# A new order for the head of a fused state-space, mixture-of-experts and attention kernel

## The reference, cut to what matters

```python
xn = layernorm(x)                                  # rows of 128
# layer 0: a long convolution plus a top-2 mixture of experts, both on xn
K  = 2 * Re(sum_n Ct[h,n] * exp(dtA[h,n] * l))     # filter of 1024 taps from log_A_real, A_imag, C, log_dt
y  = irfft(rfft(xn, 2L) * rfft(K, 2L))             # convolution over the sequence
a  = layernorm(xn + y + xn * D) * ln_w + ln_b
logits = xn @ Wg.T                                 # 8 experts, the best two are kept, softmax over the two
m  = sum over the two chosen experts e of gate_e * W3[e] @ (silu(W1[e] @ xn) * (W2[e] @ xn))
x  = x + a + m
# layer 1: attention and a dense mixture of 8 experts on layernorm(x)
x  = x + attention(layernorm(x)) + experts(layernorm(x))
```

## Time and profile before

| what | value |
|---|---|
| time, median of 3 runs | 822.92 us (822.19 to 824.34) |
| span of the profiled execution | 820.2 us |
| what lies around the span, against the median | 2.7 us |
| PE busy | 757.8 us, 92% |
| DVE busy | 658.9 us, 80% |
| ACT busy | 550.4 us, 67% |
| POOL busy | 146.5 us, 18% |
| chain that ended last | PE 75%, POOL 9%, DVE 8%, issue 4%, ACT 3% |

### The profile page before, as it was taken

One profiled execution on the slowest core, in us unless ns is written; L12 is line 12 of the kernel. 1 busy time (PEld: TensorE's weight loads), 2 busy tenths in 40 slices (PEclk: granted clock), 3 DMA queues, 4 the chain that ended last, 5 costly groups with the idle time before them and its releaser, 6 DMA issues.

```text
span 820.2 us, 11626 instructions
## 1 busy us (share of the span) xinstructions
PE 757.8 (92%) x3893; PEld 615.2 (75%) x3893; DVE 658.9 (80%) x1558; ACT 550.4 (67%) x939; POOL 146.5 (18%) x138
## 2 busy tenths in 40 slices
PE   6956366999999998999999999999999999999998
PEld 6624255888888645868788878887888887999997
DVE  7699767899937689998799889976777778877775
ACT  5833123344434368898999899889999997665663
POOL 0067775000000254643044000000000000000000
PEclk9978659899999999999999999999999999999999
DMA  8834582689876512413033112211211210000000
GB/s 251 347 104 137 185 285 90 200 250 289 291 223 195 163 40 70 86 54 89 15 102 81 40 38 59 47 43 44 55 45 49 52 27 0 14 14 20 14 20 27
DMA packets 81274, 85.15 MB, mean 104 GB/s; under 512 B 7361, under 2 KB 59841, under 8 KB 80961
## 3 DMA queue, kind: packets, MB, share of 16 engines
q1 hardware_dynamic: 77120, 76.04, 31.3%
q0 software_dynamic: 4096, 8.40, 3.5%
HBM read 59.12 MB, written 25.30 MB: 103 GB/s over the span
## 4 chain that ended last, share of the span: by engine, by line
PE 75%; POOL 9%; DVE 8%; issue 4%; ACT 3%; DMA 1%; SPq 0%; DVEq 0%; POOLq 0%
PE ps L1829 19%; PE ps L1831 18%; PE ps L1830 18%; POOL x_slots L643 9%; PE ps L1948 6%; PE ps L2024 3%; PE ps L2171 3%; DVE hid_lo L1755 2%; PE ps L1842 1%; PE ps L1927 1%; PE ps L2198 1%; PE ps L1869 1%; PE ps L1848 1%; DVE xn L1436 1%; ACT L880 1%
## 5 line engine op out<-in xcount | busy, mean ns | idle before, releaser
L1755 DVE TENSOR_TENSOR hid_lo<-hid,hid_hi 128x512 fp32r<-128x512 f32 x256 | 175.3, 686 | 52.1 <-ACT hid_hi L881 49.5
L880 ACT ACTIVATE hid<-ps,b_sb 128x512 f32<-128x512 f32 x256 | 177.7, 694 | 36.7 <-PE ps L1831 18.8
L881 ACT ACTIVATE hid_hi<-ps,b_sb 128x512 fp32r<-128x512 f32 x256 | 176.0, 688 | 0.0
L1829 PE MATMUL ps<-hid_hi,w_lo 128*128 128x512 f32 x256 | 102.1, 399 | 5.4 <-DVE hid_lo L1755 5.2
L1829 PE MATMUL ps<-xt_hi,w_lo 128*128 128x512 f32 x256 | 102.4, 400 | 1.5 <-DVE xn L1428 1.5
L1831 PE MATMUL ps<-xt_hi,w_hi 128*128 128x512 f32 x256 | 99.9, 390 | 0.0
L1831 PE MATMUL ps<-hid_hi,w_hi 128*128 128x512 f32 x256 | 99.8, 390 | 0.0
L1830 PE MATMUL ps<-xt_lo,w_hi 128*128 128x512 f32 x256 | 99.8, 390 | 0.0
L1830 PE MATMUL ps<-hid_lo,w_hi 128*128 128x512 f32 x256 | 99.8, 390 | 0.0
L792 ACT ACTIVATE act<-ps 128x512 f32<-128x512 f32 (+1 forms) x57 | 34.0, 596 | 81.6 <-PE ps L1831 81.6
L643 POOL DMA_INDIRECT x_slots<-xn,slot x64 | 71.4, 1115 | 62.6 <-DVE expert_of L1158 43.4
(11 more groups left out here) (337 smaller groups left out, 1543.9 us busy)
## 6 DMA issues: line engine op xcount, KB each, us to landing
gate_row<-gates_dram SPq DMA_DIRECT2D x64, 256.0 KB, 4.8
wc<-w_split SPq DMA_DIRECT2D x57, 256.0 KB, 3.7
w_split<-wc SPq DMA_DIRECT2D x8, 768.0 KB, 4.1
x_slots<-prod SPq DMA_DIRECT2D x11, 512.0 KB, 9.7
xc<-x_slots SPq DMA_DIRECT2D x19, 256.0 KB, 4.3
y_slots<-yo SPq DMA_DIRECT2D x19, 256.0 KB, 4.1
wst<-w SPq DMA_DIRECT2D x16, 256.0 KB, 4.7
wd<-w SPq DMA_DIRECT2D x19, 192.0 KB, 3.1
```

What stands on the lines that cost most here:

```text
L880: nc.scalar.activation(hid1[:, u % 4], ps[:, u % 4], ACT.Gelu_apprx_tanh, bias=b1_sb[:, u:u + 1])
L881: nc.scalar.activation(hid1_hi[:, u % 4], ps[:, u % 4], ACT.Gelu_apprx_tanh, bias=b1_sb[:, u:u + 1]).then_inc(hid1_done, 1)
L1755: tt(hid1_lo[:, u % 4], hid1[:, u % 4], hid1_hi[:, u % 4].bitcast(F32), sub).then_inc(hid1_lo_done, 1)
L1829: mm(dst, a_lo, b_hi, start=first, stop=False)
```

## The change

The instructions are the same; their order in the head differs, four waits are split or loosened, and six loads go to another queue.

- SP issues the eight groups of x first, then fwd0, then the zeros over x_slots, then the two raw expert weights, then the zeros over y_slots (with a semaphore of their own, spare_out), then the two small weights.
- ACT issues the small loads itself, before anything else: wg0, the two halves of log_dt, the state parameters, wqk, consts, prefix.
- PE: the product of wqk goes from the second group to behind the ranks; four numbers of spectra instead of three stand ahead of the routing's matmuls, and these no longer wait for ws_lo.
- ACT: four xt_copy before root0(0); the normalising of groups 2 to 4 follows all copies and root0(1); the filter's tanh, exp and sines go behind the gates' exponential.
- DVE: six groups of moments before scale0(0); expm1_start behind the moments; the polynomial (expm1_series) behind the choice of experts; the slots follow directly; then expm1_rest, discretise, the gates, discretise_rest.
- POOL: the scatter waits for the zeros of x_slots alone, for slots_done of 1, and group by group for the normalised rows.

The core of the diff:

```diff
@@ sync
-            for half in range(2):
-                sp.dma_start(ks[half * N:(half + 1) * N, 0, :],
-                             log_dt[half * HH:(half + 1) * HH].partition_broadcast(N)).then_inc(small_in, 16)
-            sp.dma_start(small[:], state_params).then_inc(small_in, 16)
-            sp.dma_start(wg0_sb[:], wg0).then_inc(wg0_in, 16)
             for g in range(G):
                 sp.dma_start(rows3(g), group(x, g)).then_inc(group_in[g], 16)
-                if g == 1:
-                    sp.dma_start(wqk_sb[:], wqk_t).then_inc(wqk_in, 16)
...
-            for e in range(2):
-                w0_load(e)
             sp.wait_ge(blank_done, 1)
...
+            for e in range(2):
+                w0_load(e)
...
-                         ).then_inc(blanks_out, 16)
+                         ).then_inc(spare_out, 16)
@@ gpsimd
-            pool.wait_ge(blanks_out, 16 * (-(-NC // 2) + 1))
-            pool.wait_ge(slots_done, 3)
-            pool.wait_ge(xn_ready, G)
+            pool.wait_ge(blanks_out, 16 * -(-NC // 2))
+            pool.wait_ge(slots_done, 1)
             for t in range(T):
+                if t % B == 0:
+                    pool.wait_ge(xn_ready, t // B + 1)
@@ scalar
+            act_e.dma_start(wg0_sb[:], wg0).then_inc(wg0_in, 16)
...
+            for g in range(4):
+                xt_copy(g)
             root0(0)
+            xt_copy(4)
+            normalise0(0)
+            xt_copy(5)
+            normalise0(1)
+            xt_copy(6)
+            xt_copy(7)
+            root0(1)
+            for g in range(2, 5):
+                normalise0(g)
+            spectrum_copy(0)
+            normalise0(5)
+            act_e.wait_ge(counted, 1)
...
@@ vector
-            expm1_start()
-            for g in range(5):
+            for g in range(6):
                 moments0(g, signal=(g == 3))
             scale0(0)
...
-            expm1_rest()
+            expm1_start()
             scale0(1)
...
             tt(m2, m2, m1, sub).then_inc(top2_done, 1)
-            discretise()
-            dve.wait_ge(top2_exp_done, 1)
...
+            expm1_series()
             dve.wait_ge(ranked, 1)
...
+            expm1_rest()
+            discretise()
+            dve.wait_ge(top2_exp_done, 1)
...
+            discretise_rest()
+            dve.wait_ge(ws_hi_done, 1)
@@ tensor
-                if g == 1:
-                    pe.wait_ge(wqk_in, 16)
-                    mm(ps[:, 4, 0:P], wqk_sb[:, 0], wqk_sb[:, 1], start=True, stop=True).then_inc(qk_mm, 1)
...
+            pe.wait_ge(wqk_in, 16)
             pe.wait_ge(fwd0_in, 16)
-            spectra(range(3))
+            spectra(range(4))
             pe.wait_ge(member_done, 1)
-            pe.wait_ge(ws_lo_done, 1)
...
+            mm(ps[:, 4, 0:P], wqk_sb[:, 0], wqk_sb[:, 1], start=True, stop=True).then_inc(qk_mm, 1)
-            spectra(range(3, 16))
+            spectra(range(4, 16))
```

More of the change, by code:

```diff
@@ L270, in program @@
         blanks_out = sem("blanks_out")
+        spare_out = sem("spare_out")
         member_done = sem("member_done")
@@ L528, in _ @@
                 down_load(e, q)
-            sp.wait_ge(blanks_out, 16 * (-(-NC // 2) + 1))
+            sp.wait_ge(blanks_out, 16 * -(-NC // 2))
+            sp.wait_ge(spare_out, 16)
             sp.wait_ge(blocks_known, 1)
@@ L706, in spectrum_copy @@
                 copy(z[:, m + HM * odd, c, part_], ps[:, n % 4]).then_inc(spectra_copied, 1)
[L708 to L711, removed]
-            root0(0)
-            for g in range(2, 4):
-                xt_copy(g)
-            for g in range(4):
-                normalise0(g)
-                xt_copy(g + 4)
-            root0(1)
+            act_e.dma_start(wg0_sb[:], wg0).then_inc(wg0_in, 16)
+            for half in range(2):
+                act_e.dma_start(ks[half * N:(half + 1) * N, 0, :],
+                                log_dt[half * HH:(half + 1) * HH].partition_broadcast(N)).then_inc(small_in, 16)
+            act_e.dma_start(small[:], state_params).then_inc(small_in, 16)
+            act_e.dma_start(wqk_sb[:], wqk_t).then_inc(wqk_in, 16)
+            act_e.dma_start(consts[:], lag_row.partition_broadcast(P)).then_inc(route_in, 16)
+            act_e.dma_start(prefix_sb[:], prefix).then_inc(route_in, 16)
+            for g in range(4):
+                xt_copy(g)
+            root0(0)
+            xt_copy(4)
[6 more added lines that the diff above has]
+            for g in range(2, 5):
+                normalise0(g)
+            spectrum_copy(0)
+            normalise0(5)
+            act_e.wait_ge(counted, 1)
+            copy(counts[:], ps[:, 6, 0:2 * P].rearrange("p (a t) -> p a t", a=2)).then_inc(counts_copied, 1)
+            for g in range(6, G):
+                normalise0(g)
+            for n in range(1, 4):
+                spectrum_copy(n)
+            act_e.wait_ge(top2_done, 1)
+            nc.scalar.activation(p2, m2, ACT.Exp).then_inc(top2_exp_done, 1)
             act_e.wait_ge(decay_done, 1)
@@ L724, in _ @@
             nc.scalar.activation(ks[:, 8], ks[:, 12], ACT.Sin, scale=TWO_PI / 2).then_inc(trig_done, 1)
-            for g in range(4, 6):
-                normalise0(g)
-            for n in range(2):
+            for n in range(4, 6):
                 spectrum_copy(n)
[L729 to L736, removed]
+            act_e.wait_ge(qk_mm, 1)
+            copy(ws_hi[:], ps[:, 4, 0:P]).then_inc(ws_hi_done, 1)
             act_e.wait_ge(ws_in, 32)
@@ L765, in _ @@
                 spectrum_copy(n)
-            act_e.wait_ge(blanks_out, 16 * (-(-NC // 2) + 1))
+            act_e.wait_ge(blanks_out, 16 * -(-NC // 2))
+            act_e.wait_ge(spare_out, 16)
             for c in range(KC):
@@ L990, in expm1_start, with expm1_series @@
                 need(v)
-            def expm1_rest():
+            def expm1_series():
                 v = step.mark(ts(PP, R, 1.0 / math.factorial(7), None, mul))
@@ L997, in expm1_rest @@
                     v = step.mark(stt(PP, PP, 1.0 / math.factorial(k), R, add, mul))
+            def expm1_rest():
+                need(step.n)
                 power = exp2[:].rearrange("p (a h) -> p a h", a=2)
@@ L1072, in discretise_rest @@
                 v = step.mark(ts(K(21), K(19), -1.0, None, mul))
-            expm1_start()
-            for g in range(5):
+            for g in range(6):
                 moments0(g, signal=(g == 3))
             scale0(0)
-            for g in range(5, G):
+            for g in range(6, G):
                 moments0(g, signal=(g == G - 1))
-            expm1_rest()
+            expm1_start()
             scale0(1)
-            dve.wait_ge(ws_hi_done, 1)
-            tt(ws_lo[:], ps[:, 4, 0:P], ws_hi[:].bitcast(F32), sub).then_inc(ws_lo_done, 1)
             wide = lambda a: a.unsqueeze(2).broadcast_to((P, T, E))
@@ L1089, in _ @@
             v = step.mark(tt(eq, means, wsum, mul))
-            need(v)
+            need(step.n)
             dve.wait_ge(route_in, 32)
@@ L1166, in _ @@
             ts(first_blocks[:], R_(2)[:, BLOCKS:BLOCKS + 1], 1.0, None, add).then_inc(blocks_known, 1)
+            expm1_rest()
+            discretise()
+            dve.wait_ge(top2_exp_done, 1)
+            v = step.mark(ts(p1, p2, 1.0, None, add))
+            need(v)
+            v = step.mark(nc.vector.reciprocal(p1, p1))
+            need(v)
+            step.mark(tt(gate2[:], p2, p1, mul))
+            step.mark(nc.vector.tensor_copy(xn[:, :, P], p1))
+            discretise_rest()
+            dve.wait_ge(ws_hi_done, 1)
+            tt(ws_lo[:], ps[:, 4, 0:P], ws_hi[:].bitcast(F32), sub).then_inc(ws_lo_done, 1)
             dve.wait_ge(ws_hi_done, 2)
@@ L1174, in w0_low @@
                 tt(wc[:, e % 2, :, 1], wraw[:, e % 2].rearrange("p (j w) -> p j w", j=J0), wc[:, e % 2, :, 0].bitcast(F32), sub).then_inc(w0_lo_done, 1)
-            discretise_rest()
             FH, FL, AR, CTR, CTI = K(15), K(16), K(4), K(19), K(22)
@@ L1885, in _ @@
             mm(ps[:, 7, 0:T * E], before[:], chosen, start=False, stop=True).then_inc(ranked, 1)
-            spectra(range(3, 16))
+            mm(ps[:, 4, 0:P], wqk_sb[:, 0], wqk_sb[:, 1], start=True, stop=True).then_inc(qk_mm, 1)
+            spectra(range(4, 16))
             for c in range(KC):
                 pe.wait_ge(tables_done, c // 2 + 1)
-                pe.wait_ge(k_copied, 2 * c - 2) if c >= 2 else pe.wait_ge(slots_done, 3)
+                pe.wait_ge(k_copied, 2 * c - 2) if c >= 2 else pe.wait_ge(ws_lo_done, 2)
                 for i in range(CH // HG):
```

6 lines of the change are left out of this document (2 added, 4 removed).

## The result

The changed kernel takes **826.45 us** (median of five runs, 825.76 to 829.52), beside 823.34 (822.19 to 824.34) for the kernel before on the same chip: a ratio of 1.0046, 95% interval 1.0031 to 1.0062, some 3 us slower. The forecast was 826.1.

What follows compares the result with a forecast made beforehand. DVE's filter work, from angles to chunk 1's input_low, bounds the kernel. Slots 2.8 us earlier, work behind them 6.1: angles 3.3 later, rounded to 3.2; span 823.4 plus 2.7 gives 826.1 us; range 820.8 to 829.3 (own case 825 to 828).

Steps and rivals of the forecast that it cites:

- The rival that the scatter bounds: POOL's scatter, not DVE, holds up chunk 1; its earlier end wins 3 to 4 us, giving 819.5; 3%.
- without a real pause: DVE's work runs back from chunk 1's input_low to angles at 49.12 unbroken, so all shifts as one.
- ACT's first copy and the logits: Head: seven DMA issues on ACT cost 4.6 us; copy ends at 7.3, first logits start 1.9 us earlier.
- The new wait: PE's spectra wait for ACT to normalise groups 2 and 3, until 26.3 us; advance 0.9 instead of 1.9.
- Eight matmuls instead of six: PE ahead of the count: four more passes at 0.43 make 8.7 us; count starts at 35.1 instead of 34.17.
- two more slow passes: Bound on PE's spectra in the head: the slow clock lasts longer, about 0.9 us more.
- The rival of quick passes: PE's spectra passes all take 0.43, or ACT's issues are cheap: 824.3 to 823.8; 29%.
- Behind the slots: DVE from slots to angles: expm1_rest, discretise, gates and wqk's remainder add some 6.1 us to the earlier 8.48.
- at no cost: Moved loads, POOL's lost waits, the scatter ending 2.8 us earlier or more, and wqk's move would not change the time.
- The shift of the time: Angles 3.2 us later moves the whole: span 820.2 to 823.4, median 822.92 to 826.1; 52%.
- Chunk 1 at 147.7: Chunk 1's first matmul on PE starts near 147.7 instead of 144.46, just behind DVE's input_low.
- the second sign of being wrong: The prediction is wrong if chunk 1's start no longer follows angles; the first sign was angles before 49.1.

Runs made afterwards that it cites:

- Runs 2: Kernel after with expm1_rest moved back ahead of DVE's wait for the ranks: 821.93 us, ratio 0.9987.
- run 3: Kernel after with POOL's scatter held back until ACT's four functions for discretise_rest are done: 826.03 us, ratio 1.0037.
- all nine: The kernel before, the kernel after and seven follow-up kernels, compared in one table; times from 818.91 to 826.45 us.
- runs 1: Kernel after with two numbers of spectra instead of four ahead of the routing's count on PE: 822.88 us, ratio 1.0006.
- run 5: Kernel after with two numbers of spectra ahead of the count and expm1_rest ahead of the wait for the ranks: 822.36 us, ratio 0.9993.
- run 7: Kernel after with three dense 512-column matmuls, result unused, on PE at the start: 824.82 us, ratio 1.003.

## Why the prediction was right

- **What bounds the kernel.** Right: the end follows chunk 1's input_low at the end of DVE's filter work, and not the scatter that the chain showed. Runs 2 and 3 move one without the other, and the table has it for all nine. The rival that the scatter bounds is refuted for the kernel after; for the kernel before it is read from the trace. One reading was too strong: DVE's work does not go back to angles "without a real pause". Before, DVE stood idle for 5.09 and 2.59 us ahead of the last two weight splittings, for 7.44 and 1.95 in khat, and for 0.16 at 130.18. These waits hang on work that began behind angles (in the kernel after the chain runs from DVE's splitting at 99.71 through SP's load of raw weights, 7.94 us from 102.47, to ACT's copy at 110.44), so they came later with angles, but not as one rigid block, as the sum had it.
- **ACT's first copy and the logits.** Mis-sized by half a microsecond. The seven issues took 3.9 us (0.80 to 4.71), not 4.6: the one for consts took 0.45 on ACT, where SP's 1.39 had been borrowed. The first copy so came at 6.01, not 6.7, but the logits started at 6.70, 2.5 us earlier than before instead of 1.9: they had been put at 7.3, behind ACT's copy.
- **The groups** kept their spacing: last transposes to 21.74, forecast 22.2.
- **The new wait** for ACT's normalising came as forecast: spectra at 25.79 (26.3), released by ACT after 0.83 us of idle time on PE.
- **Eight matmuls instead of six.** The sixteen passes took 9.3 us (25.79 to 35.08), not 8.7: PE ran slow a little longer than the four passes of the head before. These 0.6 us lie inside the 0.9 that had been set as a bound for two more slow passes. The spectra's start, 0.5 earlier than forecast, cancels them, and the count came at 35.08; forecast 35.1. That it fits to a tenth is luck: the same sixteen passes in the same order took 9.50 us in run 2 and 8.65 in run 3, so the moment at which the passes double their pace moves the count by some 0.8 from one execution to another. The rival of quick passes did not occur.
- **The slots** started at 37.78; forecast 37.8.
- **Behind the slots** DVE took 15.07 us to angles, where 14.6 was forecast. Slots to first_blocks 4.78 (4.74 before), expm1_rest 4.03 (3.74), discretise 1.34 (1.43), gates 0.94 (0.80), discretise_rest 3.70 (3.74), and wqk's remainder 0.28. What was mis-sized is expm1_rest and the gates: two of expm1_rest's instructions take 0.34 and 0.35, and the first of the gates 0.33 where it took 0.18. Run 3 shows what lengthens them: the scatter on POOL, which now runs beside them. With the scatter held back the stretch takes 14.49 us, as forecast. The forecast had put the earlier scatter at no cost; it costs DVE some 0.6 us (15.05 and 15.08 us in runs 1 and 7, so it is no chance of one execution). So angles came 3.73 later instead of 3.2. ACT's functions were not late.
- **The shift of the time**, 3.1 us by the medians, is the forecast's 3.2. This agreement, too, is closer than the terms are: the traces have angles 3.73 us later in the kernel after and 2.40 in run 3, whose times are alike. What lies around the span is 1.7 us here (829.52 less 827.8), and 1.7 to 1.9 in every run on record; of the 2.7 that the forecast put between span and median, some 1.0 was therefore the distance of the profiled execution before from the median.
- **Chunk 1 at 147.7** was missed in the profiled execution (152.80), for chunk 0's clock and the raw weights, which the sum took to shift along unchanged. In this trace alone chunk 1 moved by more than twice what angles did, which comes near the second sign of being wrong (chunk 1's start no longer follows angles); the medians do follow angles. That chunk 1 follows input_low, and not its rows, was right.

## What to carry to other kernels

A piece of "issue" in the chain of waits is an open question and no releaser: list what the next instruction reads, and look for the engine that delivers it last in its own order, here DVE some two microseconds after the rows had come. One trace shows which instruction the end hangs on; how far that instruction moves is read from medians, since the stretch from angles to it differed by up to 4.6 us between executions here. Releasing a wait early pays only as much as it exceeds the work that is put behind it on the same engine; work that must be done anyway belongs into the waits that stay (run 2 against the kernel after: the same slots, 4.5 us apart). Two edits that fill the same idle time do not add up (run 5), so look at how much of the wait is left before the next one. An engine that starts earlier and is off the path can still lengthen the work beside it (the scatter and DVE, 0.6 us).

## What the runs showed of the hardware

The granted clock of the head reads 1.00 in the kernels before and after, while its passes stand at twice their later spacing. The kernel after, stretches of PE (columns as above):
```profile
25.70:29.40 3.70, 3.61 (x5) 1.00 1.06 411
29.40:35.00 5.60, 5.60 (x13) 1.00 1.01 379
```
Five passes in 3.7 us and thirteen in 5.6 cannot both be at full clock (a pass on an edge counts on both sides). In run 7 the record reads 1.00 from 12 to 15 us, and it does show the fall behind the waits for ACT:
```profile
17.50:24.00 6.50, 6.03 (x28) 0.50 1.05 405
```
So in these traces a clock of 1.00 at the start of a kernel says nothing; the spacing of equal instructions does. In the kernel after PE shows no idle time from 6.70 to 24.90 us and stays at its lower level all the while, going from transposes to logits and back; in run 7, where six passes of 128x512 went before the same work, it was at the upper one until it waited for ACT.
